# Attention and routed experts on one core: order of matmuls in a half quarter, and the place of a multiply

## The reference

```python
# attention, 8 heads of 16 channels over the 128 rows; 512 queries, 512 keys
qh = layernorm(x).reshape(b, 8, 16, 512); kh = vh = ctx.reshape(b, 8, 16, 512)
s = SCALE * log(k_length)
attn = softmax(s * einsum('bhdq,bhdk->bhqk', qh, kh))
x = x + einsum('bhqk,bhdk->bhdq', attn, vh).reshape(b, 128, 512)
# experts, each of the 2048 tokens (128 a batch) through its two best of 8
z = layernorm(x)
probs = softmax(z @ gate_w.T); top 2, weights normalised
out = sum over the two of (silu(z @ w1.T) * (z @ w3.T)) @ w2.T
x = x + out
```

## Time and profile before

| | |
|---|---|
| median of 3 runs | 1259.67 us (1257.71 to 1263.73) |
| the profiled execution, its own time | 1256.96 us |
| its span in the trace | 1255.3 us |
| TensorE busy | 1073.0 us (85%) |
| VectorE busy | 811.7 us (65%) |
| GpSimd busy | 607.2 us (48%) |
| ScalarE busy | 409.5 us (33%) |
| row maxima, L715 | 256 of 1220 ns |
| exps, L592 | 512 of 598 ns |

### The profile page before, as it was taken

One profiled execution on the slowest core, in us unless ns is written; L12 is line 12 of the kernel. 1 busy time (PEld: TensorE's weight loads), 2 busy tenths in 40 slices (PEclk: granted clock), 3 DMA queues, 4 the chain that ended last, 5 costly groups with the idle time before them and its releaser, 6 DMA issues.

```text
span 1255.3 us, 19968 instructions
## 1 busy us (share of the span) xinstructions
PE 1073.0 (85%) x5113; PEld 420.3 (33%) x5114; DVE 811.7 (65%) x964; ACT 409.5 (33%) x734; POOL 607.2 (48%) x547
## 2 busy tenths in 40 slices
PE   1799999999999999851999999998999999999900
PEld 0223333333333333210444444443444444444400
DVE  5977777777777877213743965938577495953445
ACT  3266666666666666721111111111101101110100
POOL 6444666666666661222810843807466283820045
PEclk9999999999999999975999999999999999999955
DMA  6454555555555543005654755747566475743368
GB/s 181 137 180 130 162 163 163 162 162 162 162 162 162 162 130 80 35 22 184 193 101 96 222 134 164 186 100 222 129 194 174 142 201 165 186 117 85 75 190 263
DMA packets 210793, 189.57 MB, mean 151 GB/s; under 512 B 137248, under 2 KB 176160, under 8 KB 205344
## 3 DMA queue, kind: packets, MB, share of 16 engines
q1 hardware_dynamic: 197280, 120.91, 37.2%
q0 software_dynamic: 12896, 67.12, 16.4%
q10 hardware_dynamic: 576, 1.05, 0.2%
HBM read 107.50 MB, written 50.86 MB: 126 GB/s over the span
## 4 chain that ended last, share of the span: by engine, by line
PE 64%; POOL 8%; DMA 8%; DVE 7%; issue 7%; ACT 4%; SPq 1%; POOLq 0%; DVEq 0%; ACTq 0%; PEldq 0%
PE rows L1078 25%; PE heads_out L1078 13%; PE heads_out L989 7%; PE rows L962 6%; PE scores L976 6%; POOL W L433 4%; ACT W L592 4%; DVE nm L715 3%; DMA W<-parts_dram 3%; PE misc L1038 2%; POOL W L432 2%; PE misc L1059 1%; POOL U L556 1%; PE misc L1015 1%; DMA U<-U 1%
## 5 line engine op out<-in xcount | busy, mean ns | idle before, releaser
L1078 PE MATMUL rows<-W,U 128*128 x1776 | 391.6, 381 | 26.1 <-DMA U<-stage 22.8
L715 DVE TENSOR_REDUCE nm<-rows 128x2 f32<-128x1024 f32 x256 | 305.4, 1220 | 58.9 <-PE rows L962 48.4
L592 ACT ACTIVATE W<-scores 128x512 f32<-128x512 f32 x512 | 282.9, 598 | 161.8 <-PE scores L976 156.7
L1078 PEld LDWEIGHTS rows<-W,U 128*128 128x128 bf16 x1776 | 174.2, 98 | 238.4 <-issue 32.2
L661 ACT ACTIVATE U<-rows 128x512 f32<-128x512 f32 x78 | 46.4, 597 | 518.0 <-PE rows L1078 509.0
L1078 PE MATMUL heads_out<-W,U 128*128 x888 | 199.5, 381 | 14.0 <-issue 11.1
L962 PE MATMUL rows<-W,U 96*128 96x512 bf16 x512 | 163.7, 404 | 48.6 <-DMA W<-parts_dram 27.8
L976 PE MATMUL scores<-U,W 128*128 128x512 bf16 x512 | 179.6, 386 | 14.0 <-ACT W L592 4.9
L433 POOL TENSOR_TENSOR W<-U,W 128x2048 bf16<-128x2048 f32 x42 | 172.4, 4104 | 7.7 <-POOL W L432 7.7
L900 DVE TENSOR_TENSOR U<-rows,U 128x512 f32<-128x512 f32 x78 | 53.6, 688 | 182.5 <-ACT U L661 182.2
L907 DVE TENSOR_TENSOR U<-U 128x512 bf16<-128x512 f32 x78 | 161.1, 2065 | 2.7
(11 more groups left out here) (142 smaller groups left out, 677.9 us busy)
## 6 DMA issues: line engine op xcount, KB each, us to landing
U<-wpack_dram POOLq DMA_DIRECT2D x42, 1024.0 KB, 5.8
parts_dram<-U SPq DMA_DIRECT2D x32, 384.0 KB, 4.1
U<-parts_dram SPq DMA_DIRECT2D x32, 384.0 KB, 4.2
W<-parts_dram SPq DMA_DIRECT2D x32, 384.0 KB, 5.2
stage<-slots_dram SPq DMA_DIRECT2D x39, 256.0 KB, 3.0
expert_out_dram<-U SPq DMA_DIRECT2D x39, 256.0 KB, 3.1
parts_dram<-U SPq DMA_DIRECT2D x32, 256.0 KB, 4.0
stage<-wpack_dram POOLq DMA_DIRECT2D x12, 512.0 KB
```

The source lines that it names most:

```text
L592: s.activation(probs[:, w % 2, j, kk, :], sc[u % 2][:, :], ACT.Exp) \
L715: v.tensor_reduce(nm[:, bb.parity, 2 * k:2 * k + 2], p1[k % 2][:, :].rearrange("p (c k) -> p c k", c=2), AX_X, ALU.max, negate=True).then_ ...
L1078: ins = m.matmul(bank, part_of(s_part, k), W[:, bass.ds(at_w, 512)], start=(k == 0 and n == 0), stop=(k == n_chunks - 1 and n == 2))
```

## The change

Two edits. The order in a quarter becomes R s s V s s R R s s V s s R: the first row unit of each half stays ahead of the scores, the second goes behind the half's last score and whatever stands there. And the reciprocals reach the rows by one DMA that reads each head's row sixteen times into `rb` (128 x 512); the product on TensorE, its constant `selb`, and VectorE's multiply go, and GpSimd multiplies `us` by `rb` in place and adds x into `us` as well. ScalarE's copy of x1 into `xres` moves from ahead of the last three exps of a slot to behind them, and its copy into `us` waits for the z of the batch before. `rows_unit(4 * w + u // 2)` gives the same unit numbers in the same order.

```diff
                     sp.wait_ge(S["rec_out"], b.n * 16)
                     sp.nop().then_inc(S["sp_held"], 1)
                     if b.within(2, B):
-                        sp.wait_ge(S["r_ready"], b.n - 1)
-                    sp.dma_start(r8[:, :], recips_dram[bass.ds(pv.n, 1)].rearrange("o h q -> (o h) q")) \
-                        .then_inc(S["rec_in"], 16)
+                        sp.wait_ge(S["t_ready"], b.n - 1)
+                        sp.nop().then_inc(S["sp_held"], 1)
+                    sp.dma_start(rb[:, :], recips_dram[bass.ds(pv.n, 1)].rearrange("o h q -> (o h) q")
+                                 .unsqueeze(1).to_broadcast([H, DH, L])).then_inc(S["rec_in"], 16)
                 if nb.within(0, B - 1):
                     sp.wait_ge(S["m_ready"], b.n + 2)
                     sp.dma_start(maxima_dram[bass.ds(nb.n, 1)].rearrange("o s (c q) -> c (o s) q", q=P),
...
                     st.end()
                 pv = b.plus(-1)
                 if pv.within(0, B - 1):
+                    hold(S["us_ready"], b.n)
+                    hold(S["rec_in"], b.n * 16)
+                    g.tensor_tensor(us[:, :], us[:, :], rb[:, :], ALU.mult).then_inc(S["t_ready"], 1)
                     hold(S["t_ready"], b.n)
-                    if pv.within(1, B - 1):
-                        hold(S["x1_kept"], b.n - 1)
                     xr = xres[:, bass.ds(pv.n, 1), :].rearrange("p o q -> p (o q)")
-                    g.tensor_tensor(x1[:, :], xr, tb[:, :], ALU.add).then_inc(S["x1_ready"], 1)
+                    g.tensor_tensor(us[:, :], xr, us[:, :], ALU.add).then_inc(S["x1_ready"], 1)
                     hold(S["st2_ready"], b.n)
                     st = Steps(hold, S["z_steps"], pv.n, ENGINE_STEPS["z"])
                     if pv.within(2, B - 1):
...
                     st.step(g.tensor_scalar(zsc[:, 0:1], mv2[:, 1:2], EPS, 1.0, ALU.add, ALU.mult))
                     st.step(g.tensor_tensor(zsc[:, 1:2], zsc[:, 0:1], mhalf[:, :], ALU.pow))
                     st.step(g.tensor_scalar(zsc[:, 2:3], mv2[:, 0:1], -1.0, 0.0, ALU.mult, ALU.add))
-                    st.step(g.tensor_scalar(z[:, pv.parity, :], x1[:, :], zsc[:, 2:3], zsc[:, 1:2], ALU.add, ALU.mult))
+                    st.step(g.tensor_scalar(z[:, pv.parity, :], us[:, :], zsc[:, 2:3], zsc[:, 1:2], ALU.add, ALU.mult))
                     st.end()
                     g.nop().then_inc(S["z_ready"], 1)
 
...
                 if pv.within(0, B - 1):
                     act.wait_ge(S["u_ready"], b.n)
                     if pv.within(1, B - 1):
-                        act.wait_ge(S["t_ready"], b.n - 1)
+                        act.wait_ge(S["z_ready"], b.n - 1)
+                        s.nop().then_inc(S["act_held"], 1)
+                        act.wait_ge(S["x1_kept"], b.n - 1)
                     s.activation(us[:, :], misc[:, :], ACT.Copy).then_inc(S["us_ready"], 1)
                 exps(1, range(4, 8))
                 exps(2, range(6))
...
                     take_out(b, 0)
                 exps(2, range(6, 8))
                 exps(3, range(0, 5))
-                if behind:
+                exps(3, range(5, 8))
+                if pv.within(0, B - 1):
                     act.wait_ge(S["x1_ready"], b.n)
-                    s.activation(xres[:, bass.ds(pv.n, 1), :].rearrange("p o q -> p (o q)"), x1[:, :], ACT.Copy) \
+                    s.activation(xres[:, bass.ds(pv.n, 1), :].rearrange("p o q -> p (o q)"), us[:, :], ACT.Copy) \
                         .then_inc(S["x1_kept"], 1)
-                exps(3, range(5, 8))
 
             slots(act, slot)
 
...
                     v.tensor_tensor(mrow[:, 1, :], misc[0:32, 0:P], mrow[:, 0, :], ALU.subtract) \
                         .then_inc(S["m_ready"], 1)
                 maxima(range(12, 13))
-                if pv.within(0, B - 1):
-                    dve.wait_ge(S["r_ready"], b.n)
-                    dve.wait_ge(S["us_ready"], b.n)
-                    if pv.within(1, B - 1):
-                        dve.wait_ge(S["x1_ready"], b.n - 1)
-                    if ahead2.within(0, B - 1):
-                        dve.wait_ge(S["prep_done"], b.n + 3)
-                    v.tensor_tensor(tb[:, :], misc[:, :], us[:, :], ALU.mult).then_inc(S["t_ready"], 1)
                 maxima(range(13, 15))
                 if b.within(-2, -2):
                     number()
...
                     dve.wait_ge(S["x1_ready"], b.n)
                     if pv.within(1, B - 1):
                         dve.wait_ge(S["st2_ready"], b.n - 1)
-                    v.bn_stats(st2[:, :], x1[:, :]) \
+                    v.bn_stats(st2[:, :], us[:, :]) \
                         .then_inc(S["st2_steps"], 1)
                     dve.wait_ge(S["st2_steps"], b.n)
                     if pv.within(1, B - 1):
...
                         ins.then_inc(S["pv_done"], 1)
 
 
-                reader = (S["t_ready"], b.n - 1) if pv2.within(0, B - 1) else \
-                    (S["m_ready"], b.n + 1) if full else None
+                reader = (S["m_ready"], b.n + 1) if full else \
+                    (S["rank_used"], b.n - 2) if b.within(B + 1, B + 1) else \
+                    (S["us_ready"], b.n - 1) if b.within(B, B) else None
 
                 for w in range(4):
                     for u in range(8):
-                        if u % 2 == 0:
+                        if u % 4 == 0:
                             rows_unit(4 * w + u // 2)
                         if full:
                             score(w, u)
...
                                 pe.wait_ge(*reader)
                             m.transpose(misc[:, 0:P], nm[:, nb.parity, :], ident[:, :]).then_inc(S["mt_ready"], 1)
                             reader = (S["m_ready"], b.n + 2)
-                        if (w, u) == (3, 1) and behind:
-                            pe.wait_ge(S["rec_in"], b.n * 16)
-                            if reader:
-                                pe.wait_ge(*reader)
-                            m.matmul(misc[:, :], selb[:, :], r8[:, :], start=True, stop=True).then_inc(S["r_ready"], 1)
-                            reader = (S["t_ready"], b.n)
+                        if u % 4 == 3:
+                            rows_unit(4 * w + u // 2)
 
             slots(pe, slot)
             pe.wait_ge(S["og_ready"], 2 * B)
```

More of the change, by code:

```diff
@@ L122, in build @@
         us = sb("us", [P, L], F32)
-        tb = sb("tb", [P, L], F32)
-        x1 = sb("x1", [P, L], F32)
+        rb = sb("rb", [P, L], F32)
         z = sb("z", [P, 2, D], F32)
@@ L127, in build @@
         selu = sb("selu", [P, 2, P], F32)
-        selb = sb("selb", [8, P], F32)
-        r8 = sb("r8", [8, L], F32)
         den = sb("den", [P, 32], F32)
@@ L196, in build @@
             sums_out rec_out m_out den_in rec_in m_in cv_in p1_ready p1_used scores_ready exp_done pv_done
-            og_ready vt_ps vt_ready u_ready us_ready r_ready t_ready x1_ready x1_kept zt_ps zt_ready
+            og_ready vt_ps vt_ready u_ready us_ready t_ready x1_ready x1_kept zt_ps zt_ready
             gate_ready gate_used mask_ready rank_ready rank_used idx_ready rec_ready st1_steps
@@ L200, in build @@
             chunk2_steps w_ready tab_ready zero_out tiles_done x_hi x_lo up_ready silu_done h_ready
-            h_hi h_lo yb_ready pool_held dve_held sp_held gexp_ready comb_steps comb_done out_done
+            h_hi h_lo yb_ready pool_held dve_held sp_held act_held gexp_ready comb_steps comb_done out_done
             attn_done routed cnt_ready zero_ready tables_done cv_zero table_prep""".split()
@@ L223, in slots @@
                 body(Batch(b // 2, b % 2, b, b))
-        N_CONST = 10
+        N_CONST = 9
         block = cx.enter_context(nc.Block())
@@ L405, in constants @@
                 g.memset(selu[:, :, :], 0.0).then_inc(k, 1)
-                g.memset(selb[:, :], 0.0).then_inc(k, 1)
                 g.memset(ltri[:, :], 1.0).then_inc(k, 1)
                 g.memset(vt, 0.0).then_inc(k, 1)
-                hold(k, 5)
+                hold(k, 4)
                 g.affine_select(out=ident[:, :], in_=ident[:, :], compare_op=ALU.not_equal, fill=1.0, base=0,
@@ L415, in constants @@
                                     pattern=[[-32, H], [-1, DH]], channel_multiplier=1).then_inc(c, 1)
-                v = selb[:, :].rearrange("p (h d) -> p h d", h=H)
-                g.affine_select(out=v, in_=v, compare_op=ALU.not_equal, fill=1.0, base=0,
-                                pattern=[[-1, H], [0, DH]], channel_multiplier=1).then_inc(c, 1)
                 g.affine_select(out=ltri[:, :], in_=ltri[:, :], compare_op=ALU.is_gt, fill=0.0, base=0,
```

## The result

The changed kernel takes 1286.58 us (median of 5, 1279.24 to 1290.11) against 1259.07 us before (5 runs): ratio 1.0206, 95% interval 1.0169 to 1.0243. It is 2.1% slower. The profiled execution, its fastest, took 1279.24 us with a span of 1277.6 us, and against before's 1255.3 us the span's 22.3 us lie where the change is: the last transposes of z begin at 587.55 instead of 564.31 us (+23.2), the rest of the span is 0.9 us shorter than before. The median is 7.3 us above this execution. No trace of the four slower ones is kept; their clock over the whole span was 0.930 to 0.935, against 0.937 here, so more time at the low clock is the likely reason, which is not shown.

A forecast was written before the change was run, and what follows sets the result against it. Two paths were taken to bind within 1% of a slot: TensorE with ScalarE, and a round through VectorE and GpSimd. 6.4 - 3 - 0.5 - 2.7 = about 0, clock +8 on 1256.96 gives 1265; forecast 1266, range 1252 to 1282.

The forecast's parts named there:

- the term for the clock: TensorE's clock falls while it waits ahead of transposes of z: 5.5 of eleven slots at 1.4 us, +8.
- the round: Closed loop over one slot: transposes of z, gate, VectorE's routing, GpSimd's scatters and keys, x1, statistics, z; 31.28 us before.
- TensorE's own path: Quiet half quarter: values, score pair, two exps, score, values; 2.94 us forecast, from 3.32 with a row unit.
- The sum of a round: Change per loop slot: +0.38 - 0.1 + 1.1 - 0.5 - 0.33 = +0.6 us, in eleven slots +6.4.
- transposes to gate: On TensorE, two row units stand between transposes of z and gate instead of one: +0.38 us.
- gate to the end of the keys: VectorE's sixth maximum gets its unit 0.53 us later, but a later 0.69 us wait goes: net -0.1.
- keys to the end of x1: On GpSimd, a multiply is added ahead of x1's add, behind the key steps: +1.1 us, bounds +0.8 to +1.4.
- the 3 us of gain that I had written for the first slots: Slots before the routing starts, bound by TensorE's path: shorter half quarters and no product on TensorE, together -3 us.
- Edges: Slots 13 and 14: -0.5 us together; slot 15: -2.3; slot 16: -0.4, between -1 and +0.5.
- Rival (c): Clock falls in every slot, 2.5 us each (+27), and the wide DMA lands after the keys: 1272 to 1288, chance 0.16.
- Rival (a): The round binds and TensorE's clock stays full in the loop: 1257 to 1262 us, chance 0.23.
- Rival (b): TensorE's path wins, GpSimd having time for x1: slots about 29.5 us, time 1234, partly so 1246 to 1253; chance 0.13.

The follow-up runs named there:

- the fill: The changed kernel with nine score-shaped matmuls, results overwritten, where TensorE waits for z: 1259.42 us, ratio 0.9987 to the kernel before.
- the moved key steps: The changed kernel with GpSimd's key steps ahead of the wait for idx and the two scatters, not behind: 1243.10 us, ratio 0.9869 to the kernel before.

## Why the prediction was wrong

The forecast was 1266 with a range to 1282; measured was 1286.6. The direction and the mechanism held, the term for the clock was sized too small.

What binds: right in the main. In the changed kernel the round sets the slot and TensorE waits for it. On TensorE's own path a quiet half quarter came to 2.88 us where 2.94 was forecast. What I had wrong is that the order alone would leave the round as long as it was: it shortened the round too, and the slots took 30.79 us instead of 31.28.

The sum of a round, +0.6 us: measured +0.54 and +0.14 in slots 2 and 3 of the changed kernel, at full clock, +0.47 a slot with the fill. The terms of slots 5 to 11 with the fill, each beside its forecast: transposes to gate +0.33 (+0.38); gate to the end of the keys -0.32 (-0.1); keys to the end of x1 +1.30 (+1.1); x1 to statistics -0.50 (-0.5); z to transposes -0.33 (-0.33). That is +0.50 with the rest. Two terms were 0.2 off against each other, so the total is better than its parts by some luck. In detail: the multiply and the hold took 1.26 and 0.27, as assumed; VectorE waited 2.15 for x1, which starts the statistics 0.03 after it; transposes 0.18 after z. From transposes to gate it was 2.75 with the clock full, against 2.81. TensorE's wait for z was 2.3 us where I wrote "some 3".

GpSimd against VectorE for a multiply: 1.26 to 1.29 us on GpSimd, beside 0.69 on VectorE in the earlier trace rows: 1.83 to 1.87 times.

The wide DMA: 3.8 us in slot 16 (issued 577.09, multiply at 580.89) and 4.5 in slot 13, where I took 2.6 from the earlier trace rows; where the multiply waited openly in other runs, 3.6 to 4.9. So a plain load of the same size was too short a measure for it; no run here changes how the DMA reads, so what makes it longer isn't shown. In the loop the DMA was covered, as predicted, though with some 1 us or less left rather than 2 (issued at 230.73, keys done 235.74). At the start it wasn't: in slot 1 the multiply waited for it from 101.15 to 105.06, and of the 3 us of gain that I had written for the first slots 0.9 remained.

Edges: slot 13 +0.75, 14 -1.30, 15 -2.42, 16 -0.02, together -3.0; predicted -3.2.

The clock: this is the step that failed, twice. First the number of slots. I took half of eleven, as "between none and all"; the clock fell at each of the ten waits from slot 4 to slot 13. The earlier trace rows spoke for more than half: there the clock fell after a stretch in which TensorE was busy 2.05 of 3.4 us, and the stretch that I forecast, and that came, has 0.39 of 3.4 in the loop. Nothing in the trace spoke for half. Two waits escaped: 2.20 us ahead of the transposes at 143.10 (0.67 busy of the 3.4 us before them), and 2.36 us ahead of those at 514.50 (1.04 busy). Why they did is open, for the clock fell with 0.91 busy in slot 4 and 0.73 in slot 13, and in another run with 1.27. Second the price. I had 1.4 us a slot, at most 2.5, since "the remaining slots' path after the gate runs on VectorE and doesn't feel it". From transposes to the end of gate it did cost 1.7 (4.49 at 243.03 instead of 2.74 at 143.10). That was inside my bounds. But the low clock reached beyond it in every second slot: there the path from gate to idx took 15.8 us instead of 14.1 to 14.2, and the lines at 121.83 and 256.24 show how. VectorE waits 2.19 us for the sixth unit of rows instead of 0.71, because TensorE's work between gate and that unit ran at half clock until 250.6 us (the eight matmuls of the values took 1.94 us at 247.88, and 1.06 at full clock at 146.00): the unit, which the new order had put behind the sums product, was read 8.7 us after G instead of 7.2. I had seen that this unit had lost its slack and did not join the two thoughts. The nine slots took 34.24 us as a mean against 31.75 with the fill: 2.5 us of clock in each, 22.4 us in all, where the sum had 8.

So the failed step is the term "5.5 x 1.4 = +8": it measured 22.4, in nine slots at 2.5. With 22.4 in place of 8, and 2 more for the first slots, the sum is 1281 for the profiled execution, which took 1279.24. The median, 1286.58, is 5 us above that sum, and for those 5 us there is no trace.

Rival (c), the slower side, had the low clock in every slot at 2.5 each: that was right in price and nearly in place (nine of the eleven slots), with a chance of 0.16, and the median lies in its range; its second half, a DMA that lands late in the loop, did not happen in the changed kernel. In slot 4 of the kernel with the fill it did, for 2.2 us. Rival (a), the full clock at 1257 to 1262, is what the kernel with the fill shows (1259.42). Rival (b) needed a shorter round, and the moved key steps gave it one: there slots went to 30.2.

## What to carry to other kernels

Follow the waits until they close on themselves, over engines and over the loop's end: an engine that is idle a third of the time can have no time to give at the place where the round passes (GpSimd was busy 20.20 of 32 us, and 2.2 us more of it ahead of x1 cost 1.5 us a slot). Two paths bound together here within 1% of a slot, and shortening the one turned into a wait of 2.2 to 2.4 us on the other; on TensorE ten of twelve such waits cost the clock of the work behind them, 2.5 us a slot. Look in such a place for work to put in the wait (0.5 us a slot were left of the loss with nine matmuls in it), or shorten the other path first (slots of 30.2 us). And price a low clock on everything that TensorE hands over in the stretch after the wait, most of all where the same change has used up the slack: here the path from transposes to gate took 1.7 us more, and in every second slot the path from gate to idx another 1.6.

## What the runs showed of the hardware

- The clock fell at ten of twelve waits of 2.2 to 2.4 us for z, with TensorE busy 0.39 us (in slot 4 0.91, in slot 13 0.73) of the 3.4 before the transposes; it stayed full after one of 2.20 (0.67 busy) and one of 2.36 (1.04 busy). With nine matmuls in the wait (2.33 busy of 3.4) it stayed full; with four (1.25 to 1.56 busy) it fell twice in the loop, with 1.43 and 1.41 busy.
- Shorter waits were mixed. With the order alone (0.5 to 1.1 us for z) and with the reciprocals alone (0.7 to 0.9) the clock never fell between 100 and 530 us. With VectorE's multiply and the wide DMA it fell at five of twelve waits of 1.6 to 2.3 us for exps. With the reciprocals and the key steps moved, in the old order, it fell three times beside waits of 0.90 to 0.92 us for z (1.32, 1.55 and 1.73 busy of the 3.4 before). Neither the length of the last wait nor the busy time of that stretch alone tells the cases apart.
- Nine matmuls whose results nobody reads made a kernel 27 us (2.1%) faster.
- The falls kept step with the loop: slots of 35.0 and 33.3 us in turn, 68.3 together, with some 7 and 3.4 us of low clock.
- A DMA of 256 KB from DRAM, each head's row of 2 KB read sixteen times, took 3.6 to 4.9 us from its issue until the instruction that waited openly for it (3.8 and 4.5 in the changed kernel, 4.40 in the loop with the reciprocals and the key steps moved in the old order), where a plain load of the same size took 2.6 to its landing in the earlier trace rows.
